# Interleaving two sums of inner products in the first chunk of each layer, by half of the input tiles

## The reference, cut to what matters

```python
# x: 8 x 256 tokens of 1024 values, float32
def layer(x):                        # for l in 0, 1, with weights of their own
    c = x @ W_cond.T + b_cond + scale * (x @ A[id].T) @ B[id].T      # adapter of rank 16
    logits = c @ W_router.T
    w = top2_normalised(softmax(logits))                             # 8 experts
    h = einsum('td,erd->ter', c, lora_A)                             # rank 16 each: 128 columns
    f = c @ W_ffn.T + b_ffn + SCALING * einsum('ter,eor,te->to', h, lora_B, w)
    return x + f
```

## Time and profile before

| | |
|---|---|
| median of 3 runs | 680.99 us (680.96 to 681.32) |
| the profiled execution | 681.37 us, span 679.70 us from the first to the last instruction |
| granted TensorE clock | 1.00 of full speed over the whole span (2.4 GHz) |
| TensorE busy | 673.0 us, 99% |
| VectorE, ScalarE, GpSimd busy | 69%, 33%, 35% |
| W products (L607) | 1344 matmuls, 310.1 us |
| adapters' products (L567) | 128 matmuls, 30.9 us |

### The profile page before, as it was taken

How to read it: one execution, slowest core, us unless ns; L and a number is a source line. 1 busy time by engine, 2 the same in 40 slices (tenths; PEclk the granted TensorE clock), 3 DMA queues, 4 the chain that set the end, 5 groups by cost and what they waited for, 6 DMA issues and landing times.

```text
span 679.7 us, 9094 instructions
## 1 busy us (share of the span) xinstructions
PE 673.0 (99%) x3243; PEld 592.9 (87%) x3243; DVE 467.6 (69%) x724; ACT 226.6 (33%) x429; POOL 238.7 (35%) x201
## 2 busy tenths in 40 slices
PE   8999999999999999999999999999999999999997
PEld 7999999888788888888899999998887888888886
DVE  5664667888969495955673743788798757959533
ACT  6445244644121034211524343255441402242100
POOL 2373023025096070068133433030513932400960
PEclk9999999999999999999999999999999999999999
DMA  8345756993829954466742745679937498636623
GB/s 297 109 153 189 257 193 211 393 378 117 279 92 321 381 164 146 156 195 211 288 164 74 246 149 195 247 245 381 365 96 260 158 342 310 178 102 192 209 96 124
DMA packets 73988, 147.17 MB, mean 217 GB/s; under 512 B 6932, under 2 KB 38164, under 8 KB 73814
## 3 DMA queue, kind: packets, MB, share of 16 engines
q1 hardware_dynamic: 70534, 138.12, 59.1%
q10 hardware_dynamic: 1872, 6.36, 3.0%
q0 software_dynamic: 1536, 2.10, 1.1%
HBM read 98.34 MB, written 47.33 MB: 214 GB/s over the span
## 4 chain that ended last, share of the span: by engine, by line
PE 75%; DMA 9%; DVE 8%; POOL 3%; SPq 2%; issue 2%; ACT 1%; POOLq 0%; ACTq 0%
PE ps L607 33%; PE ps L492 13%; PE ps L493 12%; PE ps L494 12%; DMA form_scratch<-f_hl 4%; PE ps L567 2%; DMA x_raw<-in_xT 2%; DMA x_raw<-x_scratch 2%; PE ps L613 2%; POOL w L1393 2%; DVE x_hl L982 2%; POOL c L1405 1%; DVE f_hl L982 1%; DMA e_raw<-in_ext 1%; DVE x_raw L1207 1%
## 5 line engine op out<-in xcount | busy, mean ns | idle before, releaser
L607 PE MATMUL ps<-x_hl,a_hl 128*128 128x512 f32 x1344 | 310.1, 390 | 0.8 <-ACT w L901 0.6
L607 PEld LDWEIGHTS ps<-x_hl,a_hl 128*128 128x128 f32 x1344 | 252.2, 188 | 54.1 <-ACT w L901 1.5
L492 PE MATMUL ps<-e_hl,w_hl 128*128 128x384 f32 (+1 forms) x432 | 146.0, 338 | 0.7 <-DVE e_hl L982 0.6
L493 PE MATMUL ps<-e_hl,w_hl 128*128 128x384 f32 (+1 forms) x432 | 145.7, 337 | 0.0
L494 PE MATMUL ps<-e_hl,w_hl 128*128 128x384 f32 (+1 forms) x432 | 145.5, 337 | 0.0
L492 PEld LDWEIGHTS ps<-e_hl,w_hl 128*128 128x128 f32 x432 | 81.2, 188 | 2.6 <-issue 1.3
L493 PEld LDWEIGHTS ps<-e_hl,w_hl 128*128 128x128 f32 x432 | 81.2, 188 | 0.0
L494 PEld LDWEIGHTS ps<-e_hl,w_hl 128*128 128x128 f32 x432 | 81.2, 188 | 0.0
L982 DVE TENSOR_TENSOR x_hl<-x_raw,x_hl 128x512 fp32r<-128x512 f32 x64 | 70.5, 1154 | 3.9 <-ACT x_hl L805 3.8
L1417 POOL TENSOR_TENSOR x_raw<-x_raw,u 128x512 f32<-128x512 f32 x16 | 20.7, 1315 | 136.3 <-DVE u L985 136.3
L1393 POOL TENSOR_TENSOR w<-x_raw 128x512 f32<-128x512 f32 x16 | 25.6, 1633 | 107.3 <-DMA x_raw<-in_xT 33.3
(11 more groups left out here) (124 smaller groups left out, 896.1 us busy)
## 6 DMA issues: line engine op xcount, KB each, us to landing
a_hl<-form_scratch SPq DMA_DIRECT2D x112, 512.0 KB, 5.8
form_scratch<-f_hl SPq DMA_DIRECT2D x56, 512.0 KB, 7.3
e_raw<-in_ext SPq DMA_DIRECT2D x12, 580.0 KB, 8.9
w_raw<-in_w ACTq DMA_DIRECT2D x12, 512.0 KB, 3.4
x_raw<-in_xT SPq DMA_DIRECT2D x6, 1024.0 KB, 9.4
x_raw<-x_scratch SPq DMA_DIRECT2D x6, 1024.0 KB, 9.2
x_scratch<-x_raw SPq DMA_DIRECT2D x16, 256.0 KB, 3.0
out_T<-x_raw SPq DMA_DIRECT2D x16, 256.0 KB, 3.2
```

What stands on the lines that cost most here:

```text
L492: nc.tensor.matmul(dst, w_hi, m_hi, start=start, stop=False, skip_group_check=again)
L493: nc.tensor.matmul(dst, w_hi, m_lo, start=False, stop=False, skip_group_check=again)
L607: last = nc.tensor.matmul(ps[:, bank, :], a_hl[:, n % NM, k, w, :], x_hl[:, slot, k, x, :], start=start and i == 0, stop=i == 3 * KH - 1, ...
```

## The change

In the first chunk of each layer (`g % SUPER == 0 and tb == 0`, two of the eight calls of `routers`) the two sums are no longer made one after the other. TensorE makes the adapters' products of B11's four tiles (8 matmuls), the experts' of the same (12), the adapters' of B21's (8), where `pe_s` is counted, and the experts' of B21's (12), where `pe_hx` is counted. The wait for `hg_done` stands between the first two. In the other six calls the order stays. Each sum still adds its tiles in the same order.

```diff
--- before.py
+++ after.py
@@ -560,20 +560,37 @@
                 if u:
 
                     pe.wait_ge(S["logit_read"], u)
-                for k in range(KT):
-                    block = blocks[k // KH]
-                    pe.wait_ge(x_lo[block], KH * g + k % KH + 1)
-                    for hl in range(2):
-                        last = nc.tensor.matmul(ps[:, S_BANK, :], s_hl[:, k, :],
-                                                x_hl[:, slots[block], k % KH, hl, :],
-                                                start=(k + hl == 0), stop=(k + hl == KT))
-                last.then_inc(S["pe_s"], 1)
-                if u:
-                    pe.wait_ge(S["hg_done"], u)
-                for k in range(KT):
-                    slot = slots[blocks[k // KH]]
-                    last = split_product(ps[:, H_BANK, :], px_hl[:, k, 0, :], px_hl[:, k, 1, :],
-                                         x_hl[:, slot, k % KH, 0, :], x_hl[:, slot, k % KH, 1, :], k == 0, False)
+                def adapters_of(ks):
+                    for k in ks:
+                        block = blocks[k // KH]
+                        pe.wait_ge(x_lo[block], KH * g + k % KH + 1)
+                        for hl in range(2):
+                            last = nc.tensor.matmul(ps[:, S_BANK, :], s_hl[:, k, :],
+                                                    x_hl[:, slots[block], k % KH, hl, :],
+                                                    start=(k + hl == 0), stop=(k + hl == KT))
+                    return last
+
+                def experts_of(ks):
+                    for k in ks:
+                        slot = slots[blocks[k // KH]]
+                        last = split_product(ps[:, H_BANK, :], px_hl[:, k, 0, :], px_hl[:, k, 1, :],
+                                             x_hl[:, slot, k % KH, 0, :], x_hl[:, slot, k % KH, 1, :], k == 0, False)
+                    return last
+
+                def bank_free():
+                    if u:
+                        pe.wait_ge(S["hg_done"], u)
+
+                if g % SUPER == 0 and tb == 0:
+                    adapters_of(range(KH))
+                    bank_free()
+                    experts_of(range(KH))
+                    adapters_of(range(KH, KT)).then_inc(S["pe_s"], 1)
+                    last = experts_of(range(KH, KT))
+                else:
+                    adapters_of(range(KT)).then_inc(S["pe_s"], 1)
+                    bank_free()
+                    last = experts_of(range(KT))
                 last.then_inc(S["pe_hx"], 1)
 
             def inner_low(l, g, tb):
```

## The result

The changed kernel takes 682.68 us (median of 20 runs, 681.67 to 684.72), the kernel before beside it 681.13 (680.05 to 682.81). The medians lie 1.55 apart. The profiled execution took 682.01 us with a span of 680.3, 0.6 above the span before.

The account below looks back on a forecast made before the run. TensorE, working 99% of the span, was taken as the bound. Layer 0's +0.21 and layer 1's +0.51 us sum to +0.72 on the median 680.99, giving 681.7 us, range 680.9 to 682.8.

Parts of the forecast that it names:

- The saving at the splits: Products ahead of W1: late B21 splits no longer stop TensorE, saving 0.38 us in layer 0, 0.22 in layer 1.
- The moved chain: Adapters' sum to routing on ScalarE and VectorE: routing's first transpose starts 1.33 (layer 0) and 1.48 us (layer 1) later.
- the W3 m1 wait in layer 1: Sign of a right forecast: TensorE's wait for the second w57 copy gone in layer 1, paying nothing instead of 0.50.
- The new wait: Before W2 m0 TensorE waits for the first u2 copy: 1.24 us in layer 0, 1.23 in layer 1.
- What gives it back: Later waits, W2 m3's ring tile and W3 m1, shrink: layer 0 regains 0.46 and 0.41 us, layer 1 0.50.
- the ring tile: W2 m3's wait for its DMA in layer 0: disappears because the DMA doesn't move, giving back 0.46 us.
- layer 1's give-back: W3 m1 in layer 1: TensorE arrives past the w57 copy's end, so 0.50 us comes back, layer +0.51.
- the cost that the trace of before did not show: VectorE's moved hg_hl against GpSimd's first B22 step: 0 to 0.44 us in layer 0, 0.22 taken; layer 1 nothing.
- The first: Rival: no wait before W2 m0 because ScalarE's and VectorE's chains catch up; 681.0 us, at best 680.4; chance 0.12.
- The second: Rival at W3 m1: the w57 copy moves with TensorE, so the lag stays, 1.41 us, time 682.4; chance 0.15.
- The third: Rival: B21's splits still stop TensorE, adding at most 0.60 us to the lag, time 681.9; chance 0.03.

Follow-up runs that it names:

- Experiment 2: Changed kernel with three tiles' experts' products, then one tile's, between the adapters' halves (9 and 3 matmuls instead of 12): +0.5 and +0.3 us against the kernel before.
- after_w5first: Changed kernel with ScalarE's second W5 copy into w57 moved ahead of the hg cast: +0.5 us against the kernel before.
- late_sum: Kernel before in its old order, but pe_s counted only behind 12 experts' matmuls in the two changed calls: +1.4 us against the kernel before.
- one_tile: Changed kernel with one tile's experts' products (3 matmuls instead of 12) between the adapters' halves: +0.3 us against the kernel before.
- before_w5first: Kernel before with only ScalarE's second W5 copy moved ahead of the hg cast: -1.2 us against the kernel before, -0.6 in a second comparison.
- before_both: Kernel before with ScalarE's first two u2 copies ahead of the exp and second W5 copy ahead of the hg cast: -0.8 us against the kernel before.
- after_u2first: Changed kernel with ScalarE's first two u2 copies placed ahead of its exp: +0.6 us against the kernel before.

## Why the prediction was right, and where its sizes were off

**The saving at the splits.** Forecast 0.38 and 0.22, seen 0.33 and 0.17: the 40 matmuls take 9.12, not 9.07. The forecast took the one profile's losses as fixed. In the ten stages profiled in the old order W1 started anywhere from 9.12 to 10.13; what ended those waits was each time VectorE's split of a tile of B21, and ScalarE's casts ahead of these had waited for the tokens' DMA.

**The moved chain.** Right. Routing starts 1.45 and 1.61 later, counted from the stage's start (forecast 1.33 and 1.48). VectorE still stands 0.87 for lb_hl, as the forecast had it, and takes the sum 0.07 after ScalarE, which is part of the 0.12 missed. The u2 copy was found where it was put, behind the gap. Of the signs that were to show the forecast right the W3 m1 wait in layer 1 failed: it was to be gone, and cost 0.36. Routing in layer 1 was a little past its 1.3 to 1.5, and the others came. No new wait came in the later chunks.

**The new wait.** Forecast 1.24 and 1.23 for each, idle time plus what the next matmuls lose. Measured in layer 0: the group after inner_low starts at 135.82, so W2 m0's turn is at 141.26 and the matmul behind W2's 48 has its turn at 152.14; that first low-rank matmul starts at 153.44. That is 1.30. The lateness of the copy was 1.11 (142.37 against 141.26), so the rule drawn from the earlier trace rows, lateness plus 0.2, held on a wait that did not exist before. Experiment 2 then scaled it.

**What gives it back.** The mechanism is right and is the one that matters. All 26 stages obey one rule within 0.1 us: the stage is the larger of two paths, TensorE's (its first low-rank matmul behind W2, plus 34.90) and the w57 copy's (its end, plus 2.93). Where that copy is moved ahead of the hg cast, only the first path is left. The two constants are read off the stages in which one path clearly decides (34.90 from after_w5first, layer 0; 2.93 from before, layer 0). Seven of them:

| stage | TensorE's path | w57's path | measured |
|---|---|---|---|
| before, layer 0 | 67.01 | 64.82 + 2.93 = 67.75 | 67.75 |
| before, layer 1 | 66.41 | 64.00 + 2.93 = 66.93 | 66.91 |
| after, layer 0 | 67.53 | 64.78 + 2.93 = 67.71 | 67.69 |
| after, layer 1 | 67.54 | 64.96 + 2.93 = 67.89 | 67.91 |
| late_sum, layer 0 | 68.17 | 65.19 + 2.93 = 68.12 | 68.22 |
| late_sum, layer 1 | 68.16 | 64.33 + 2.93 = 67.26 | 68.16 |
| one_tile, layer 0 | 66.23 | 63.60 + 2.93 = 66.53 | 66.51 |

Before, the copy decides; after, the two are within 0.4. Layer 0, term by term: -0.33 at the splits, +1.30 for the new wait, -0.46 at the ring tile, -0.58 at W3 m1 (0.15 instead of 0.73), together -0.07. The forecast was +0.21. That layer 0 came out at nothing is luck in part: the copy came no later only because the tokens came sooner, as the next paragraph shows.

**The step that was mis-sized** is layer 1's give-back: "TensorE comes 1.01 late, at 520.44, past the copy's end, and pays nothing instead of 0.50". TensorE came 1.14 later, the copy 0.96 later, and W3 m1 paid 0.36, so 0.14 came back and not 0.50: -0.17 + 1.31 - 0.14 = +1.00 against a forecast of +0.51, and with it the sum, 0.72 against 1.1 (0.6 to 1.6). Two assumptions were wrong. First, the end of the copy was taken as fixed. It is fixed to B22's tokens, and these move: GpSimd starts on them between 26.42 and 29.36 us after the stage's start in these profiles. In layer 1 it was 27.22 before and 27.76 after, in layer 0 28.05 and 27.57, so layer 0 got 0.48 as a present and layer 1 paid 0.54. Nothing in the change issues or moves a DMA, and within each order the starts differ by more than that (by 1.3 us in the ten stages of the old order, by 2.9 in the 16 with experts' products moved). But that the reorder delays the tokens a little isn't excluded: the mean is 27.40 over the ten and 27.81 over the 16, with a standard deviation of 0.5 and 0.8. Second, the cost that the trace of before did not show. I had allowed 0 to 0.44 in layer 0 (0.22 in the sum) and nothing in layer 1; it came in both, 0.45 each. VectorE's hg_hl step and GpSimd's steps in the changed kernel, layer 0, and the same in layer 1:

```profile
148.38 6.39 POOL L1410 TENSOR_TENSOR w<-x_raw 128x512 f32<-128x512 f32 x4 [32.85 <-DMA x_raw<-in_xT]
154.74 6.83 POOL L1422 TENSOR_TENSOR c<-w,x_raw 128x512 f32<-128x512 f32 x4
...
148.85 1.37 DVE L999 TENSOR_TENSOR hg_hl<-hg,hg_hl 128x512 fp32r<-128x512 f32 x1 [0.69 <-ACT hg_hl L902]
150.15 6.87 DVE L999 TENSOR_TENSOR x_hl<-x_raw,x_hl 128x512 fp32r<-128x512 f32 x4
```

```profile
483.14 6.38 POOL L1410 TENSOR_TENSOR w<-x_raw 128x512 f32<-128x512 f32 x4 [33.05 <-DMA x_raw<-x_scratch]
489.49 6.83 POOL L1422 TENSOR_TENSOR c<-w,x_raw 128x512 f32<-128x512 f32 x4
...
483.44 1.55 DVE L999 TENSOR_TENSOR hg_hl<-hg,hg_hl 128x512 fp32r<-128x512 f32 x1 [0.69 <-ACT hg_hl L902]
484.91 6.87 DVE L999 TENSOR_TENSOR x_hl<-x_raw,x_hl 128x512 fp32r<-128x512 f32 x4
```

The T2 steps (output c) take 6.83 together, where they took 6.38 before:

```profile
155.51 6.38 POOL L1405 TENSOR_TENSOR c<-w,x_raw 128x512 f32<-128x512 f32 x4
```

VectorE's hg_hl (0.69 when alone) starts during GpSimd's first step and stretches to 1.37 and 1.55; GpSimd's T3 steps do not get longer, but VectorE is one step further behind: its last B22 split ended during the first T2 step before (34.98 after the stage's start, T2's second step began at 36.09), and now it reaches into the second (36.2 against 35.62), which takes 1.73 instead of 1.29. I had reasoned that a later VectorE costs nothing; it costs the same 0.45, only further on. Where VectorE comes first, GpSimd pays at once. That case is in before_w5first, layer 0:

```profile
148.13 6.88 POOL L1394 TENSOR_TENSOR w<-x_raw 128x512 f32<-128x512 f32 x4 [32.12 <-DMA x_raw<-in_xT]
...
148.07 0.69 DVE L983 TENSOR_TENSOR hg_hl<-hg,hg_hl 128x512 fp32r<-128x512 f32 x1 [0.69 <-ACT hg_hl L885]
```

6.88 for the T3 steps instead of 6.38. Over all 26 stages profiled the rule is plain: where GpSimd starts after hg_hl has ended (12.0 us after routing's start), both groups take 6.4. Where it starts during hg_hl, T3 grows with the overlap: by 0.50 for 0.64, by 0.25 for 0.37 (before_both, layer 1), by 0.05 for 0.18. Where it starts ahead of hg_hl, T2 grows by 0.45. Two stages where GpSimd was 1.5 us or more ahead of hg_hl (late_sum and after_u2first, layer 1) have T3 at 6.05 and 6.08 and T2 at 6.83, so net 0.1. The change moves routing, and hg_hl with it, 1.45 us into the time when B22's tokens arrive. The rule of the Trainium skill in "SBUF — State Buffer", section "Who interferes with whom", that the order of issue decides which of the two is blocked, agrees with both orders in these rows: the step of the one who came second is the one that is stretched, VectorE's from 0.69 to 1.37, GpSimd's first from 1.29 to 1.79. The price for w57's copy is nearly the same either way (0.45 and 0.50), since it hangs on the end of T2.

From GpSimd's start to the end of w57's copy it is 36.77 where neither group is stretched (before, layer 0: 64.82 - 28.05). So for an average arrival (27.65 over the 26 stages) w57's path is 27.65 + 36.77 + 2.93 = 67.35 before, and 0.45 more, 67.80, after, with TensorE's path at 67.53: +0.45 for each layer, +0.9 for both. The interval of the measurement, 0.6 to 1.6, holds that; the forecast's 0.7 is in it too, so the times alone do not decide between the two, the profiles' stages do. Corrected like this, after the result, the sum no longer needs the single profile's B22 times.

**The rivals.** The first (no new wait) is out: there are 2.0 us of it. The second (the lag isn't given back, 682.4, +0.21%) did not happen by its mechanism: w57's copy stayed tied to GpSimd's start, as the rule over the 26 stages shows. Its time, 1.4 above the kernel before, is inside the interval all the same. The third is out: no weight load of the split stage waits for VectorE in the changed kernel.

## What to carry to other kernels

Before moving work ahead of a handover, follow what is queued behind its readers on their own engines: here a copy that had nothing to do with the sum stood behind them, with 0.66 us to spare, and 12 matmuls went ahead where 3 would have hidden the late tiles. A saving upstream of a wait that another chain ends is no saving; look for that wait first (here one line in ScalarE's order was worth 0.6 to 1.2 us, the reorder nothing that could be told). Here a second such limit stood right behind the first, and both moved with one transfer: the ring tile and GpSimd's work both follow the landing of B22's tokens. And where a decision rests on when a DMA lands, take its spread over several profiles, not the one value.

## What the runs showed of the hardware that was not expected

- GpSimd's start on B22's tokens had a spread of 2.9 us over 13 profiles and two layers (26.42 to 29.36 us after the stage's start), and the wait for the ring tile of W2 m3 went from nothing to 0.75 us, with the same order of DMAs. The tile is issued right behind the tokens, and the two are late together: GpSimd's start plus 4.06 us gives the first matmul behind W2 within 0.05 us wherever the tile is what TensorE waits for.
- TensorE that waits for a copy loses the lateness and 0.2 us more, in six waits (0.73 and 0.50 before; 1.30 and 1.31 after, for copies 1.11 and 1.12 late; and in the changed kernel's W3 m1 0.15 and 0.36, for copies 0.04 early and 0.13 late).
- Two streams of two-input steps on VectorE and GpSimd take turns at 1.70 us a pair, and one step of VectorE too many costs GpSimd 0.45 us when GpSimd comes first and 0.50 when VectorE does.
